# Next query features before the attention's product, and the first tile's edge sums between denominators and gate, in a graph-transformer layer

## What is computed

```python
xn = layernorm(x)
# graph part: mean of xn over each node's incoming edges
neigh = segment_sum(xn[src], dst, 6250) / maximum(deg, 1)
g = layernorm(xn @ W_self.T + neigh @ W_neigh.T + bias) * gamma + beta
# linear attention over all nodes, 8 heads of 64
q = elu(xn @ Wq.T / 8) + 1
k = elu(xn @ Wk.T) + 1
a = (q @ (k.T @ v)) / (q @ k.sum(0) + 1e-8)      # per head
x = x + g + a @ W_out.T + b_out
# mixture of experts: 2 shared, 8 routed, the best 2 taken per node
x = x + shared(layernorm(x)) + routed(layernorm(x))
```

## Time and profile before

| | us |
|---|---|
| median of 3 runs | 3106.45 (3105.29 to 3109.77) |
| the profiled execution, its time | 3111.14 |
| its span, from the first to the last instruction | 3109.5 |
| TensorE busy (of it) | 2428.8 |
| VectorE busy | 1534.8 |
| GpSimd busy | 1290.3 |
| ScalarE busy | 1090.0 |

### The profile page before, as it was taken

One profiled execution on the slowest core, in us unless ns is written; L12 is line 12 of the kernel. 1 busy time (PEld: TensorE's weight loads), 2 busy tenths in 40 slices (PEclk: granted clock), 3 DMA queues, 4 the chain that ended last, 5 costly groups with the idle time before them and its releaser, 6 DMA issues. The chain is left out here.

```text
span 3109.5 us, 46892 instructions
## 1 busy us (share of the span) xinstructions
PE 2428.8 (78%) x13332; PEld 1489.2 (48%) x13333; DVE 1534.8 (49%) x3736; ACT 1090.0 (35%) x2118; POOL 1290.3 (41%) x1370
## 2 busy tenths in 40 slices
PE   5989767777777777777777777777776799988999
PEld 3545434444444444444444444444444566665776
DVE  7889623444444444444443444443446344444666
ACT  3556533232333333333332333332322343432333
POOL 4656655444434443434444443433430232223443
PEclk9999977777777777777777777777777899998999
DMA  8466455444444444444444444444443454446676
GB/s 278 146 213 203 137 157 179 149 149 141 136 138 139 146 144 141 144 142 147 143 148 148 148 138 137 146 132 129 148 138 133 138 164 160 162 149 191 241 260 213
DMA packets 190001, 497.26 MB, mean 160 GB/s; under 512 B 42012, under 2 KB 54812, under 8 KB 188152
## 3 DMA queue, kind: packets, MB, share of 16 engines
q0 software_dynamic: 92720, 309.47, 33.9%
q1 hardware_dynamic: 66505, 135.52, 12.8%
q10 hardware_dynamic: 30719, 51.60, 4.4%
HBM read 373.91 MB, written 122.50 MB: 160 GB/s over the span
## 5 line engine op out<-in xcount | busy, mean ns | idle before, releaser
L614 POOL DMA_INDIRECT Wff<-table,ebuf x225 | 228.7, 1016 | 544.7 <-DMA ebuf<-edges 482.7
L614 POOL DMA_INDIRECT region<-table,ebuf x225 | 225.5, 1002 | 447.0 <-DMA ebuf<-edges 369.0
L654 POOL DMA_INDIRECT region<-table,idx x122 | 116.9, 958 | 358.6 <-PE bank L1298 265.5
L323 PE MATMUL bank<-Wff,region 128*125 128x512 f16 (+1 forms) x636 | 246.0, 387 | 13.9 <-DVE region L2012 7.3
L324 PE MATMUL bank<-Wff,region 128*125 128x512 f16 (+1 forms) x636 | 244.4, 384 | 0.0
L325 PE MATMUL bank<-Wff,region 128*125 128x512 f16 (+1 forms) x636 | 243.8, 383 | 0.0
L1137 PE MATMUL bank<-region,ohs 128*125 128x512 f16 x850 | 233.9, 443 | 8.9 <-issue 8.8
L1871 DVE SCALAR_TENSOR_TENSOR region<-bank,sv,bias_bc 125x512 f32<-125x512 f32 x50 | 37.5, 751 | 403.5 <-PE bank L325 229.0
L1137 PE MATMUL bank<-Wff 128*125 128x512 f16 x850 | 235.0, 446 | 0.0
L621 POOL DMA_INDIRECT region<-table,ebuf x200 | 192.8, 964 | 60.9 <-issue 60.9
L621 POOL DMA_INDIRECT Wff<-table,ebuf x200 | 191.0, 955 | 60.9 <-issue 60.9
(11 more groups left out here) (322 smaller groups left out, 5901.7 us busy)
## 6 DMA issues: line engine op xcount, KB each, us to landing
yd<-region ACTq DMA_DIRECT2D x59, 512.0 KB, 3.0
x2d<-region SPq DMA_DIRECT2D x25, 512.0 KB
table<-region SPq DMA_DIRECT2D x25, 512.0 KB
region<-x2d SPq DMA_DIRECT2D x25, 512.0 KB
table<-region POOLq DMA_DIRECT2D x50, 250.0 KB, 3.4
xnt<-region POOLq DMA_DIRECT2D x25, 500.0 KB, 4.0
region<-xnt SPq DMA_DIRECT2D x25, 500.0 KB
x2t<-region SPq DMA_DIRECT2D x25, 500.0 KB
```

Source lines behind the costliest of these rows:

```text
L323: wmm(ps, xh, wh, start=first, stop=False)
L614: pool.indirect_dma_start(out=ring[j][:, s, :], out_offset=None, in_=table, in_offset=bass.IndirectOffsetOnAxis(ap=ebuf[j][:, 2 * s:2 * s ...
L654: pool.indirect_dma_start(out=tg[:, c, :], out_offset=None, in_=table2, in_offset=bass.IndirectOffsetOnAxis(ap=idx[:, 2 * turn + c:2 * tur ...
```

## The change

On TensorE the query features become a function of their own, `queries(i)`. Those of group 0 are made before the first group; those of the next group are made inside a group, between the spread of the denominators and the attention's product. The edge sums of the next group's first tile move from behind the spread to between the denominators and the gate. On SyncE the load of the next group's transposed rows moves from behind the first tile's edge list to in front of it. The other engines' lists stay as they are.

```diff
@@ block.sync, group(i, prev, nxt, later)
                 if prev is not None:
                     store_normalised(prev)
+                if nxt is not None:
+                    load_xt(nxt)
                 if later is not None:
                     edge_steps(later, 0)
                 if nxt is not None:
-                    load_xt(nxt)
                     load_x(nxt)
                 store_x2(i)
@@ block.tensor
-            def group(i, prev, nxt):
-
+            def queries(i):
                 pe.wait_ge(sem["xt_in"], 16 * (i + 1))
                 if past(i):
                     pe.wait_ge(sem["h_sb"], 2 * i)
...
                     if c % 2:
                         last.then_inc(sem["q_ps"], 1)
+
+            def group(i, prev, nxt):
...
                 last.then_inc(sem["den_ps"], 1)
+                if nxt is not None:
+                    aggregate(nxt, 0)
                 if prev is not None:
                     gate(prev)
                 pe.wait_ge(sem["q_rec"], 2 * i + 2)
...
                     last.then_inc(sem["spread_ps"], 1)
                 if nxt is not None:
-                    aggregate(nxt, 0)
+                    queries(nxt)
...
             pe.wait_ge(sem["mf_set"], KC)
+            queries(0)
             group(0, None, 1)
```

## The result

The changed kernel takes 3172.77 us (3170.1 to 3186.35 over three runs), 1.0204 of the kernel before, 95% interval 1.0162 to 1.0246: slower by 66 us. The forecast was 3175. The profiled execution is the slowest of the three, 3186.35 us, so the traces lie 75 us apart and not 66.

The account below looks back on a forecast made before the run. TensorE bounds the stage, losing time in issue gaps under gather bursts. Terms -0.8 - 0.7 + 1.9 + 2.6 = +3.0 us for some 23 group borders: +69 us, 3175 us on the median; range 3020 to 3310 us.

Parts of the forecast that it names:

- five marks for the profile after: Signs expected: no reciprocal wait, 2 to 3 us before first mean's transposes, another before second's, issue gaps in attention, none in features.
- Edge sums ahead of gate and spread: TensorE before the spread: the moved sums hide the wait for VectorE's reciprocal, minus 0.8 us a group.
- What TensorE does under the first burst: First tile's gathers: slightly more matmul work in hand when the crawl starts, 3.9 us for 3.2, minus 0.7 us a group.
- s + 9: Nine us after s, the start of the first tile's gathers; TensorE was to crawl from s + 6 to about s + 24.
- The mean behind the attention: Before the first mean's transpose: features no longer cover VectorE's residual and count and ScalarE's mean, plus 1.9 us a group.
- VectorE a stage later: Before the second tile's mean: VectorE needs 16.2 us after the attention, TensorE 13.6, so plus 2.6 us a group.
- The lower bound's reason: For the second mean's wait: 0 if the half clock stretches TensorE's side as it did for 16 of these matmuls.
- Loads: SyncE's transposed rows asked for earlier: delay of one DMA issue, 0.35 us, hidden by the ring's slack; priced at nothing.
- A milder first burst: Rival: fewer other transfers under the first gathers shrink TensorE's loss, -4.3 us x 23 = -99 us, 3007 us; chance 0.27.
- The spread's signal stuck: Rival: slow stretch begins before s + 4, VectorE's scaling waits until s + 24, +12 us a group, about 3450 us; chance 0.13.
- Moves covered: Rival: the new waits stay hidden, within 6 us of before, or -0.8 us a group, 3088 us; chance 0.15.
- The rule on instruction fetch: Other explanation of the first gap: a taken branch to an unbuffered page forces a fetch, so the gap stays at the loop's head.

Follow-up runs that it names:

- The experiment with the bounds moved: Changed kernel with the two register loads of the second tile's edge loop ahead of the wait for the first mean: 1.0489 of the kernel before.
- the last: Changed kernel with the first tile's mean and the next queries' negative and positive parts made earlier on VectorE and ScalarE: 0.9791 and 0.9762 of the kernel before.
- the changed kernel again: The changed kernel, unaltered, rerun when the kernel before took 2383 us and showed no slow stretch under the gathers: 1.0715 of the kernel before.
- the run of the features alone with the mean early: Changed kernel with edge sums put back behind the spread and the first tile's mean taken earlier on VectorE and ScalarE: 1.0507 of the kernel before.
- the run with the mean first: Changed kernel with the first tile's mean moved behind the reciprocal on VectorE and ahead of the queries' high parts on ScalarE: 1.0373 of the kernel before.

## Why the prediction was right, point by point

The sum was right, +3.0 us a group for +3.3 measured, but by luck in part: two of its four terms came out near what was written (-0.8 and +1.9), one near in size with the picture behind it wrong (-0.7), and one didn't appear (+2.6); losses that the sum didn't have made up for it. Of the five marks for the profile after, the first held (no wait for the reciprocal), the second nearly (1.8 us ahead of the first mean's transposes for 2 to 3), and three failed: no wait ahead of the second mean's transposes, few issue gaps in the attention's lines (7.9 us in all), and nearly as many as before in the features' (251 us for 267).

- *Edge sums ahead of gate and spread*, -0.8: the wait is gone. The sections up to the spread gained 1.3 in all.
- *What TensorE does under the first burst*, -0.7: measured -0.4. The picture behind it failed. I had the features done at s + 9 and the attention crawling. In the group shown the burst starts at 1218.5 and the features at 1222.3, s + 3.8 as forecast, but the crawl takes hold at 1226.4: at 0.107 us each 21 of them ran up to s + 6 and 18 after it, not 32. So 9 were left for the stretch, the issue gaps stayed in the features' lines, and the attention came behind. Counted in all groups up to the first gap of over 0.2 us, 17 to 38 matmuls ran past s + 6 (median 24), and in the kernel before 20 to 39 (median 31), so the group shown is at the low end, and the number in hand is no constant. Nor were there 32 in the group that the prediction read: the places were through by s + 6, and 21 features ran before the crawl, with six more in pairs up to 1213.5. Why fewer matmuls were in hand was not tried.
- *The mean behind the attention*, +1.9: measured 1.8. Its consequence was left out: the blocked instruction stream didn't load the next loop's bounds ahead, 1.4 us more. The experiment with the bounds moved shows the cause.
- *VectorE a stage later*, +2.6: measured 0 in the changed kernel. The lower bound's reason fits what the windows show, the second tile's sums stretched to 11.1 us by the lower clock, together with TensorE's two new stops ahead of them; this is read from the trace and was not tried. The term itself was no fiction: once the first mean is early the second one's wait appears, at 1.6 and 3.3 us a group in two of the experiments and at 2.5 in 18 groups of the last.
- In its place stands what was not in the sum, the attention at the lower clock, +2.4, and the second tile's sums, +1.0, less 1.5 us in the neighbour part. Why the second slow stretch cost less was not tried.
- *Loads*, 0: shown in the quick condition.
- *The rivals.* A milder first burst: wrong, 13.4 us idle for 12.8, though the load and the two other large transfers left it and what the DMA engines moved fell from 260 to 196 GB/s. Its price was also added up wrongly: it takes 3.5 us for the mean terms, which the sum has at 4.5, so 3030 us and not 3007. The spread's signal stuck: it didn't happen, spread to features 1.9 us. Moves covered: wrong for the mean. The rule on instruction fetch of the Trainium skill ("Runtime: NRT & Kernel Launch", Instruction fetch mechanics) asked for a gap at the loop's head, which would now be the mean's transposes; the changed kernel's gaps stayed with the gathers and with the features, and the 1.4 us of issue at the head are the register loads, so the trace doesn't agree with that rule as their cause.

What makes TensorE crawl under a burst stays open. It isn't the gathers alone: GpSimd issues them at the same pace in both conditions (L622, mean 955 ns into the second tile's ring in both runs of the changed kernel, 956 and 1020 into the first's), and in the quick one there is no gap. Nor is it TensorE's alone: in the changed kernel's slow stretch VectorE too starts its small operations only every 2 us, with nothing shown that it waits for; in the changed kernel again the same two follow one another without a gap.

```profile
1232.62 0.23 DVE L1704 TENSOR_TENSOR ohc<-Wff,ohs 128x125 f16<-128x125 f16 x1 [1.89 <-issue]
1234.73 0.23 DVE L1705 TENSOR_SCALAR iota_f<-iota_f 128x125 f32<-128x125 f32 x1 [1.89 <-issue]
```

## What to carry to other kernels

When a matmul block moves ahead of another on the engine that sets the time, ask what the block covered where it stood: here 48 feature matmuls behind the attention gave VectorE and ScalarE the time to turn the attention's result into the next group's inputs. Removing the wait that shows then only uncovers the next link of the same chain; the order on the helper engines has to be changed with it (inputs of the next group first, then the norm). With that the two changes together paid, 2% in the slow condition; in the quick one it wasn't measured. A short wait or a run of narrow matmuls ahead of wide ones is to be priced with the clock behind it: 0.8 us of waiting for the reciprocal and the gate's narrow matmuls went with 2 us in the sums that followed.

## What was not expected of the hardware

- One kernel, one chip, two conditions that lasted over a set of runs: 2385 us in one set and 3116 in another, with no change in the kernel. The difference lies in the slow stretches under the gathers (features 20.7 or 5.1 us a group, neighbour part 26.1 or 13.2). The same edit is worth +2.0% in the one and +7.2% in the other. The wait for the mean is 1.8 us a group in the one and 4.6 in the other, so the stretch probably also gives late helpers time; that was not tried.
- Two register loads showed no gap where TensorE's stream ran ahead of its matmuls, and gaps of 0.5 to 1.7 us a group behind a blocking wait; the first of them took from 0.30 to 1.8 us.
- The clock under full load after a short rest: in the run of the features alone with the mean early, the first tile's sums, behind the gate and 0.8 us of waiting for the reciprocal, took 10.1 us (445 ns a matmul) and the second's, with no wait ahead, 8.1 (380 ns). It also fell with no rest at all, behind the gate's 24 matmuls of 8 columns and the spread, in the changed kernel again (granted clock 0.50 from 1243.0 to 1248.4, above). In the run with the mean first, TensorE waited 2.1 us for the relu, and soon after it had begun again its wide matmuls went from 0.38 to 0.63 us:

```profile
1216.86 0.43 PE L323 MATMUL bank<-Wsn,region 128*125 128x512 f16 x1 [2.08 <-ACT region L877]
...
1217.35 0.38 PE L325 MATMUL bank<-Wsn,region 128*125 128x512 f16 x1
...
1217.79 0.63 PE L324 MATMUL bank<-Wsn,region 128*125 128x512 f16 x1
```
